# Attention values on four column tiles: the order of the matmuls, tile by tile instead of in turn

## What is computed

```python
# cross-attention of the layer, H = 16 heads, D_K = 16
q, k, v = x @ Wq, ctx @ Wk, ctx @ Wv            # split into 16 heads
p = softmax(q @ k.T / sqrt(D_K))                # (16 heads, 256 tokens, 120 context rows)
o = p @ v                                       # (16 heads, 256 tokens, 16)
out = o.reshape(256, 256) @ Wo
```

## Time and profile before

| | |
|---|---|
| median of 3 runs | 1987.2 us (1986.87 to 1988.95) |
| profiled execution, its own time | 1987.2 us |
| its span in the trace | 1985.3 us |
| TensorE matmul busy | 1381.7 us (70%) |
| VectorE busy | 1274.3 us (64%) |
| GpSimd busy | 999.9 us (50%) |
| ScalarE busy | 755.7 us (38%) |
| mean granted clock of TensorE | 0.839 |

### The profile page before, as it was taken

One profiled execution on the slowest core, in us unless ns is written; L12 is line 12 of the kernel. 1 busy time (PEld: TensorE's weight loads), 2 busy tenths in 40 slices (PEclk: granted clock), 3 DMA queues, 4 the chain that ended last, 5 costly groups with the idle time before them and its releaser, 6 DMA issues. The chain is left out here.

```text
span 1985.3 us, 28570 instructions
## 1 busy us (share of the span) xinstructions
PE 1381.7 (70%) x6660; PEld 945.6 (48%) x6661; DVE 1274.3 (64%) x3248; ACT 755.7 (38%) x2416; POOL 999.9 (50%) x1214
## 2 busy tenths in 40 slices
PE   6504558700025766667766899998499999999997
PEld 5403446500014554445545667776355555555554
DVE  4599999999989999999987134353322322322322
ACT  5422223501102664565777478886311111111111
POOL 3238888886669997877777425332112112112111
PEclk9757778955557887787887899998699999999999
DMA  4601113520030100010001211143130410411200
GB/s 125 210 5 33 44 38 99 181 106 0 0 132 27 31 26 21 21 36 25 26 26 39 94 32 57 42 137 117 53 110 21 161 58 21 158 61 44 85 16 6
DMA packets 97685, 125.41 MB, mean 63 GB/s; under 512 B 10001, under 2 KB 74952, under 8 KB 95560
## 3 DMA queue, kind: packets, MB, share of 16 engines
q1 hardware_dynamic: 60040, 97.22, 15.3%
q10 hardware_dynamic: 33136, 18.58, 3.2%
q0 software_dynamic: 4432, 8.73, 1.2%
HBM read 89.68 MB, written 35.74 MB: 63 GB/s over the span
## 5 line engine op out<-in xcount | busy, mean ns | idle before, releaser
L208 POOL TENSOR_TENSOR wt<-wt 128x1024 f32<-128x1024 f32 x128 | 304.5, 2379 | 107.8 <-DVE wt L166 107.8
L214 POOL TENSOR_TENSOR wt<-wt 128x512 f32<-128x512 f32 (+2 forms) x384 | 316.9, 825 | 30.1
L1848 PE MATMUL e_ph<-wt,e_g 128*128 x624 | 274.3, 592 | 0.0
L166 DVE SCALAR_TENSOR_TENSOR wt<-wt,scan 128x256 f32<-128x256 f32 x512 | 242.5, 474 | 0.2 <-issue 0.2
L156 DVE TENSOR_TENSOR scan<-scan,wt 128x256 f32<-128x256 f32 x512 | 219.6, 429 | 20.1 <-DVE wt L166 14.0
L147 DVE TENSOR_REDUCE scan<-wt 128x16 f32<-128x272 f32 x512 | 223.2, 436 | 0.1
L135 DVE TENSOR_TENSOR wt<-wt,scan 128x256 f32<-128x256 f32 x512 | 209.9, 410 | 5.4 <-PEq L231 5.4
L1339 ACT ACTIVATE wt<-p_pX,p_mx 128x120 f32<-128x120 f32 x512 | 176.9, 390 | 79.3 <-DVE p_mx L1127 77.9
L1471 PE MATMUL p_pm<-p_w_mix,p_oT 128*128 128x256 f32 x128 | 43.6, 500 | 221.0 <-DMA p_oT<-o 190.7
L1741 POOL TENSOR_TENSOR e_ve<-e_mv,eps 128x1 f32<-128x1 f32 x39 | 7.4, 189 | 368.8 <-DVE e_mv L1792 368.8
L1848 PEld LDWEIGHTS e_ph<-wt,e_g 128*128 128x128 f32 x624 | 115.5, 190 | 130.8 <-issue 130.8
(11 more groups left out here) (220 smaller groups left out, 2920.8 us busy)
## 6 DMA issues: line engine op xcount, KB each, us to landing
wt<-in_L_ffn_W SPq DMA_DIRECT2D x24, 1024.0 KB
qkv<-f_st ACTq DMA_DIRECT2D x48, 256.0 KB, 2.3
p_kE<-kE SPq DMA_DIRECT2D x16, 480.0 KB, 3.7
p_vP<-vP SPq DMA_DIRECT2D x16, 480.0 KB
e_xt<-routed ACTq DMA_DIRECT2D x39, 130.0 KB, 2.1
f_xt<-in_x SPq DMA_DIRECT2D x16, 256.0 KB, 2.8
f_raw_k<-qkv SPq DMA_DIRECT2D x4, 1024.0 KB, 5.3
f_raw_q<-qkv SPq DMA_DIRECT2D x4, 1024.0 KB, 7.8
```

The source lines that it names most:

```text
L166: nc.vector.scalar_tensor_tensor(s["S"][:, h, u], s["S"][:, h, (u - 1) % R], s["gate"][:, jb, h, 1, bass.ds(c * R + u, 1)], s["outer"][:], ...
L208: nc.gpsimd.tensor_tensor(x, s["S"][:, h, z * Q:(z + 1) * Q], s["q"][:, h, now].rearrange("p t (o d) -> p t o d", o=1).to_broadcast([P, Q, ...
L214: nc.gpsimd.tensor_tensor(x[:, :, :, 0:half], x[:, :, :, 0:half], x[:, :, :, half:2 * half], ALU.add).then_inc(s["o_fold"][h], 1)
L1848: ins = nc.tensor.matmul(ph2[:], g1[:, c // (C1 // 2), c % (C1 // 2)], wt[:, bass.ds(at_b + (W2_AT + c * F2), F2)], start=(c == 0), stop=( ...
```

## The change

The loop over the four column tiles moves from the innermost place to the place just inside `q`. The same 32 matmuls with the same operands, flags and semaphores are issued in another order: before, four consecutive matmuls go to four different tiles; after, four consecutive matmuls go to one tile, then four to the next. Within one tile the order stays `q`, `g`, `p`. The last matmul issued is the same one.

```diff
                 for q in range(2):
-                    for g in range(G):
-                        for p in range(2):
-                            for group in range(4):
+                    for group in range(4):
+                        for g in range(G):
+                            for p in range(2):
                                 ins = nc.tensor.matmul(pq[32 * group:32 * group + 32, g, q * P:(q + 1) * P], vP[:, q, g * 4 + group, p],
                                                        prT[:, group * 4 + g * 2 + p, q * P:(q + 1) * P], start=(p == 0), stop=(p == 1))
                 ins.then_inc(pv_done, 1)
```

## The result

| | before | after |
|---|---|---|
| median, 5 runs each | 1987.2 us (1985.91 to 1990.46) | 2009.77 us (2008.70 to 2010.45) |
| profiled execution, its own time | 1987.2 us | 2008.67 us |
| its span | 1985.3 us | 2006.8 us |
| one call of `values` at full clock | 1.95 us | 4.33 us |

The ratio is 1.0106, with an interval of 1.0094 to 1.0117. On 1987.2 that is 21.1 us (18.7 to 23.3); the two medians of five differ by 22.6. I had forecast 1989.0 in a range up to 2003, so the time lies outside that range. The profiled executions differ by 21.5 us in own time and in span.

What follows compares the result with a forecast made beforehand. The scan on VectorE bound 650 to 970 us, TensorE 1181 to 1370, then chains in the drain. Nine calls paid in full, 9 x 0.2 = 1.8 us, on 1987.2 gave 1989.0 us, range 1985 to 2003.

Steps and rivals of the forecast that it cites:

- Does the order matter to TensorE?: Prediction's step on `values`: later matmuls on other tiles pass earlier ones; how far depends on instructions held, 37 to 64.
- +0.2 us a call: Chosen cost of the new order in `values`: 1.97 instead of 1.77 us, if 64 instructions count from the oldest unfinished.
- Both readings of the total: Limits on instructions TensorE holds in `values`: 64 from the oldest unfinished, +0.2 us a call; or 37 unstarted, +0.6 us.
- The row I leaned on: First two score calls: four matmuls started within 0.06 us, so tile 2's first passed at least 12 unstarted instructions.
- Strict order: The skill's rule that TensorE matmuls start and end first in, first out; the prediction held that the rows speak against it.
- the queue of 64: The skill's TensorE queue depth of 64 with a partial reorder window; by it a `values` call costs +0.2 us.
- Two or three tiles at a time: Slower rival for `values`: passing reaches between 16 and 48 instructions; 1993 us, or 2003 with two tiles; chance 0.21.
- the short reach: Sign in the profile after: 2.4 to 3.6 us from a `values` call's start to the score behind it.
- the serial tiles: Slower rival for `values`: passing under 16 instructions, tiles work one after another, 6.2 us a call, 2034 us; chance 0.15.
- the clock: Faster rival: an earlier clock rise in the drain, where all at 1.00 would be 12 us; chance 0.04.
- The floor: Claim that a `values` call cannot go below 16 x 0.109 = 1.74 us, with nothing to gain in the call itself.
- The count of calls: Nine `values` calls paid in full (972, 1016, six from 1181 to 1356, 1411); the other seven hidden.

Runs made afterwards that it cites:

- the first try: Against the kernel before, the new order in calls 1 to 6 and 9 to 12 of the sixteen, not the seven meant; 2002.71 us, ratio 1.0074.

## Why the prediction was wrong

**The step that failed** is the last one of "Does the order matter to TensorE?": "Whether they can start depends on how many instructions TensorE holds". I counted the held instructions over all tiles together, 37 unstarted or 64 from the oldest unfinished, and took it that any of them may start when its tile is free. What counts is the number waiting at each tile. With the order of before they spread over four tiles. With the new one 16 in a row go to one tile, and the sixth or seventh that finds no place there stops the stream. So +0.2 us a call came out, where the chip took +2.38. Both readings of the total fell with it: the second gave +0.6, a fourth of the measured.

TensorE held as many after as before. Its register instruction behind `values`, the answer to the earlier trace rows:

```profile
L1508 PEldq ALU_OP  x1: 36/36/36, 1228.4 to 1228.4; - x1
```

```profile
1225.57:1228.40 2.83, 2.82 (x46) 2.82 (x47) 1.00 0.00 0
```

By then 46 matmuls and 47 loads of the call had started, so 35 of its 128 had not, against 37 before. The observation was right and did not bear on the limit. Both numbers are more than the 24 that could wait on four tiles with six places each; so the rest must wait in front of the tiles, where the order is kept. This is inferred from the two counts and was not tested by itself.

**The row I leaned on could not show it.** In the earlier trace rows tile 2's first matmul passed 12 instructions, and I wrote that they were passed "with no sign of a limit". They were spread over two tiles, eight on each, two of which start at once: six waited, which just fits. The distance passed was never the measure. The experiment with two in a row puts as many on a tile and costs 0.07 us; with three it costs 1.07. Before the run, the row should have been read as "up to eight on one tile are seen to be free, and 16 are not seen".

**Strict order, and the queue of 64.** The Trainium skill ("TensorE: Matmul & The Clock Gate", Part 3) has matmuls start and end strictly first in, first out. By that a call would have been 6.2 us by my own sum, and none was: the order of before takes 1.95, and even eight in a row takes 5.95, or 5.68 to the start of its last record, which is what the 6.2 count. But the rule is half right, and I weighed it as wholly refuted: entry is in order, and only what has entered may start beside others. The queue depth of 64 for TensorE on the same page of the Trainium skill (Architectural detail) bore my +0.2. No order here was limited at 64: with three in a row the stream stops at the seventh waiting instruction or before.

**The rivals.** Two or three tiles at a time, to which I gave 0.21, is what the trace shows: two at a time. I priced two tiles at a perfect overlap, 32 x 0.109 = 3.5 us, +1.75. In fact two tiles share only 0.32 of each block's 0.79 us, which gives +2.38. It was short by 0.63 a call, 5.7 over nine calls; with the call that pays in part (1.7) that is 7.4, and 6.8 lie between 2003 and the measured 2009.8. From its start to the score behind it a call now takes 4.26 us, between the 3.6 that I had named for the short reach and the 6.3 for the serial tiles. The serial tiles would have given 6.2 us a call; the eight in a row come near it. No run shows the clock to have moved the total; single steps it may have moved both ways, as told below.

**The floor** of 16 x 0.109 per call held: no order ran below 1.95 us, so no version here beats the kernel before.

**The count of calls** held. Nine in full are 9 x 2.38 = 21.4; the one at 1087 adds 1.7, since its cover was enough for +0.2 and not for +2.38. That makes 23.1, against 21.1 (18.7 to 23.3) by the ratio, 22.6 by the medians, and 23.2 in the profiles from the first call on. The last match has luck in it: the step behind the call at 972 grew by 4.6 us and not by 2.38, and the step behind the call at 1384, which should have stayed the same, shrank by 2.2. Two more of the nine are firm in every trace. From the start of the call at 1016 to the next it is 41.0 to 41.1 us in the four kernels that run it in the new order and 37.6 to 38.8 in the three that run it in the old. From the start of the last call to the end it is 575.8 to 576.3 us in the new order and 573.5 to 574.1 in the old. The call at 1384 stayed hidden: in the timeline of after the score behind it no longer waits, and the projection waits 1.28 us in place of 2.24; it starts 6.6 us behind the start of the call before and after (1390.90 - 1384.27 and 1412.39 - 1405.78).

```profile
1405.78 4.33 PE L1536 MATMUL p_pq<-p_prT,p_vP 120*32 120x128 f32 x64
1410.03 1.08 PE L1514 MATMUL p_pX<-p_kE,p_qT 32*128 32x240 f32 x8
1412.39 1.97 PE L1471 MATMUL p_pm<-p_wo,p_aT 128*128 128x256 f32 x8 [1.28 <-ACT p_aT L1363]
```

The call at 1055 stayed hidden too (+5.2 before it and +5.1 behind it), beyond the 0.77 us of cover that I named: the projection two places on waited 3.55 us for a copy of `pq`, and waits 2.67 after. It starts 8.0 us behind the start of the call in both:

```profile
1063.13 3.32 PE L1471 MATMUL p_pm<-p_wo,p_aT 128*128 128x256 f32 x7 [3.55 <-ACT p_aT L1363]
```

```profile
1068.29 2.97 PE L1471 MATMUL p_pm<-p_wo,p_aT 128*128 128x256 f32 x8 [2.67 <-ACT p_aT L1363]
```

**What stays open.** The call at 972 can't be priced alone. From its start to the next call it is 4.6 us more after, and only 0.2 us more with the new order in the first half, where the same two calls ran. The windows of that step (columns of the earlier trace rows) in the kernel before, after (where the step ends 3 us behind the window), and with the first half changed:

```profile
972.00:1016.00 44.00, 35.96 (x236) 28.01 (x236) 38.63 (x99) 35.52 (x130) 30.55 (x39) 0.92 0.10 31
```

```profile
972.00:1016.00 44.00, 34.58 (x204) 26.97 (x199) 31.98 (x89) 32.17 (x112) 28.89 (x36) 0.88 0.10 26
```

```profile
972.00:1016.00 44.00, 34.59 (x236) 27.56 (x235) 39.40 (x99) 35.14 (x129) 29.87 (x37) 1.00 0.10 30
```

The clock granted was 0.92, 0.88 and 1.00. Whether the clock is the cause is not shown: two in a row took 46.4 us for the step at 0.85, the first try 48.8 at 0.90. But the step took 42.1 to 44.7 us in the three kernels that run this call in the old order, and 44.5 to 48.9 in the four with the new one. So a single profile can't price this call, and only the sums over runs bear on it. Also open is whether the room is five or six, whether it counts loads, matmuls or both, and whether it is the same for row tiles and for other types than float32.

## What to carry to other kernels

When small matmuls run on several tiles of the array, issue them to the tiles in turn; two float32 matmuls in a row on a tile cost 0.07 us here on a call of 1.95, three 1.07 and four 2.38. When a profile shows instructions passing others, ask how many of those passed belong to one tile before the reach is extended to a new order. A cover has a size: a call that was hidden at +0.2 us may pay at +2.4, so price the covers again for the upper bound of the cost.

## What the runs showed of the hardware

- In six orders of float32 matmuls a column tile of TensorE behaved as if it had room for five or six waiting instructions (or three matmuls, which fits as well); the stream enters in order, and a full tile stops it for all tiles. The next tile began with five left waiting in blocks of 12, 16 and 32 instructions.
- Where nothing stops it, entry is quick: with two float32 matmuls (eight instructions) in a row, all four tiles had begun within 0.05 us.
- Total instructions held, 37 before and 35 after, did not tell the fast order from the slow one.
- The clock granted to the step from 972 to 1016 us was between 0.88 and 1.00 in kernels that differ there in little or nothing.
